# A quarter of the folded W_down summed elementwise ahead of its multiply, and first inputs loaded by halves on two queues, in a gated block with a decay scan and a gated MLP

## What is computed

```python
x = x + tanh(g_xattn[0]) * wkv(w, u, _layernorm(x), ctx)     # x, ctx: (8, 128, 256)
# wkv, for each batch and channel, over the 128 steps, in effect:
#   y_t = (sum_(s<t) e^((t-1-s) w + k_s) v_s + e^(u + k_t) v_t) / (the same without v)
x = x + tanh(g_ffn[0]) * ffn(_layernorm(x))
# ffn: a = fwht(n * SU_ug) / 64                                # 256 channels
#      h = silu(a @ W_gate.T * s_gate * 64) * (a @ W_up.T * s_up * 64)   # 1024 channels
#      out = fwht(h * SU_dp) / 64 @ W_down.T * (Wscale_dp * 64)
```

## Time and profile before

| | us |
|---|---|
| median of 3 runs | 106.79 |
| lowest, highest | 106.39, 107.57 |
| the profiled execution | 106.32 |
| its span | 104.4 |

### The profile page before, as it was taken

One profiled execution on the slowest core, in us unless ns is written; L12 is line 12 of the kernel. 1 busy time (PEld: TensorE's weight loads), 2 busy tenths in 40 slices (PEclk: granted clock), 3 DMA queues, 4 the chain that ended last, 5 costly groups with the idle time before them and its releaser, 6 DMA issues.

```text
span 104.4 us, 2022 instructions
## 1 busy us (share of the span) xinstructions
PE 95.8 (92%) x714; PEld 89.4 (86%) x714; DVE 70.2 (67%) x155; ACT 63.7 (61%) x140; POOL 52.3 (50%) x75
## 2 busy tenths in 40 slices
PE   0189999999999999999999999999999999999990
PEld 0148788759688999999999999999999999999980
DVE  0389989979999987999995689795325331412341
ACT  4497837978968744999477168937546432234310
POOL 5068697331999079530724927076493234322310
PEclk9999999999999999999999999999999999999999
DMA  1998999910000000000002000000200000020002
GB/s 58 293 272 257 397 393 401 365 71 6 0 0 0 0 6 0 0 0 0 0 0 105 5 0 0 0 9 0 100 0 0 0 6 0 0 100 0 0 0 100
DMA packets 3585, 7.69 MB, mean 74 GB/s; under 512 B 340, under 2 KB 760, under 8 KB 3576
## 3 DMA queue, kind: packets, MB, share of 16 engines
q1 hardware_dynamic: 3576, 7.57, 20.6%
HBM read 6.52 MB, written 1.05 MB: 73 GB/s over the span
## 4 chain that ended last, share of the span: by engine, by line
PE 86%; DMA 7%; SPq 3%; DVE 1%; issue 1%; DVEq 0%
PE UG L1046 45%; PE OD L1097 14%; PE KZ L1097 8%; DMA XT<-in_xt 7%; PE UG L961 3%; PE FX L1016 3%; PE FX L989 2%; PE UG L955 2%; PE FX L1001 2%; PE UG L975 1%; PE KZ L925 1%; PE UG L940 1%; PE VB L1026 1%; PE VB L1031 1%; PE VB L1038 1%
## 5 line engine op out<-in xcount | busy, mean ns | idle before, releaser
L437 POOL TENSOR_TENSOR HL<-H,HH 128x256 fp32r<-128x256 f32 x31 | 24.8, 807 | 27.6 <-ACT HH L703 27.6
L892 DVE SCALAR_TENSOR_TENSOR H<-S,ALPHA,UG 128x256 f32<-128x256 f32 x32 | 15.3, 478 | 19.0 <-ACT S L712 18.9
L712 ACT ACTIVATE S<-UG,CV 128x256 f32<-128x256 f32 x32 | 15.1, 472 | 13.5 <-PE UG L1046 13.5
L1046 PE MATMUL UG<-FH,WTH 128*128 128x256 f32 x128 | 21.8, 292 | 0.2 <-DVE FH L856 0.2
L1046 PE MATMUL UG<-FL,WTH 128*128 128x256 f32 x128 | 21.0, 286 | 0.0
L1046 PE MATMUL UG<-FH,WTL 128*128 128x256 f32 x128 | 20.5, 283 | 0.0
L1046 PEld LDWEIGHTS UG<-FH,WTH 128*128 128x128 f32 x128 | 17.7, 191 | 1.6 <-issue 0.8
L1046 PEld LDWEIGHTS UG<-FL,WTH 128*128 128x128 f32 x128 | 17.7, 191 | 0.5 <-issue 0.5
L1046 PEld LDWEIGHTS UG<-FH,WTL 128*128 128x128 f32 x128 | 17.6, 191 | 0.0
L703 ACT ACTIVATE HH<-H 128x256 fp32r<-128x256 f32 x32 | 13.2, 413 | 2.8 <-DVE H L892 2.6
L1097 PE MATMUL OD<-HH,MH 128*128 128x256 f32 x40 | 11.3, 283 | 0.0
(11 more groups left out here) (145 smaller groups left out, 191.1 us busy)
## 6 DMA issues: line engine op xcount, KB each, us to landing
WN<-in_weights SPq DMA_DIRECT2D x4, 512.0 KB, 9.4
DN<-in_w_down SPq DMA_DIRECT2D x2, 512.0 KB, 8.5
out<-XT SPq DMA_DIRECT2D x3, 256.0 KB, 2.4
X<-in_x SPq DMA_DIRECT2D x2, 256.0 KB, 3.4
V<-in_ct SPq DMA_DIRECT2D x2, 256.0 KB, 6.8
XT<-in_xt SPq DMA_DIRECT2D x2, 256.0 KB, 8.8
V<-in_ct SPq DMA_DIRECT2D x1, 512.0 KB, 9.2
X<-in_x SPq DMA_DIRECT2D x1, 512.0 KB, 10.4
```

Of the source, the lines that this page charges most:

```text
L437: eng.tensor_tensor(HL[:, q % JT, 0:n], ring(H, q), HH[:, q % JT, 0:n].bitcast(F32), ALU.subtract).then_inc(done, 1)
L712: act.activation(ring(S, q), gate_part(q), ACT.Silu, scale=VT[:, V_SGATE + j:V_SGATE + j + 1]).then_inc(silu_ready, 1)
L892: dve.scalar_tensor_tensor(out=ring(H, q), in0=ring(S, q), scalar=ALPHA[:, j:j + 1], in1=up_part(q), op0=ALU.mult, op1=ALU.mult).then_inc( ...
L1046: return pe.matmul(dst, w[:, m, j, t, :], f[:, g, t, :], start=start, stop=stop, skip_group_check=True)
```

## The change

SUMMED gets the second quarter: fly(9) is made, and its two matmuls become one. The lists of all four engines are reordered, before block 0 and up to block 22. x of group 0 and the constants are loaded in two halves by partitions, one from SP and one from ScalarE, and SP's later loads change their order. All waits on const_in and on x_in of group 0 ask for both halves; only two of them are shown.

```diff
@@ -42,15 +42,15 @@
 
 TURNED = (0, 1,)
 
-SUMMED = (2, 3)
+SUMMED = (1, 2, 3)
 
 LATE = (SLOTS - 1,)
 
 
 PE_STAGES = {
-    -1: [("busy", 0), ("center", 0), ("keys", 0), ("busy", 1), ("busy", 2), ("w", 0), ("fwht_x", 0), ("busy", 3), ("busy", 4),
-        ("keys", 1), ("w", 1), ("w_rest", 0), ("busy", 5), ("w", 2), ("fwht", 0), ("w", 3), ("w_rest", 1), ("ones", 0), ("m", 0),
-        ("spread", 0), ("w_rest", 2), ("w_rest", 3)],
+    -1: [("busy", 0), ("busy", 1), ("center", 0), ("keys", 0), ("w", 0), ("fwht_x", 0), ("busy", 2), ("busy", 3), ("w", 1), ("w", 2),
+        ("keys", 1), ("w_rest", 0), ("busy", 4), ("w_rest", 1), ("busy", 5), ("fwht", 0), ("w", 3), ("ones", 0), ("w_rest", 2), ("m", 0),
+        ("spread", 0), ("w_rest", 3)],
     0: [("keys", 2), ("m", 1)],
     2: [("m", 2)],
     3: [("m", 3)],
@@ -61,61 +61,61 @@
     12: [("fwht", 2)],
     13: [("ones", 2)],
     14: [("spread", 2)],
-    20: [("fwht", 3)],
-    21: [("ones", 3)],
-    22: [("spread", 3)],
+    18: [("fwht", 3)],
+    19: [("ones", 3)],
+    20: [("spread", 3)],
 }
 ACT_STAGES = {
-    -1: [("setup", 0), ("rows", 0), ("signs", 0), ("steps", 0), ("tanh", 0), ("decay", 0), ("keys", 0), ("gated", 0), ("ratio", 0),
-        ("recip", 0), ("w_hi", 0), ("w_lo", 0), ("keys", 1), ("w_hi", 1), ("w_hi", 2), ("square", 0), ("w_hi", 3), ("w_hi", 4),
-        ("f_copy", 0), ("w_hi", 5), ("w_lo", 1), ("w_lo", 2), ("w_lo", 3), ("m_hi", 0), ("norm1", 2), ("recip", 1), ("keys", 2)],
+    -1: [("setup", 0), ("rows", 0), ("tanh", 0), ("signs", 0), ("steps", 0), ("decay", 0), ("keys", 0), ("ratio", 0), ("recip", 0),
+        ("w_hi", 0), ("w_hi", 1), ("w_hi", 2), ("gated", 0), ("keys", 1), ("square", 0), ("w_lo", 0), ("w_hi", 3), ("w_hi", 4),
+        ("f_copy", 0), ("w_lo", 1), ("w_lo", 2), ("w_lo", 3), ("norm1", 2), ("recip", 1), ("m_hi", 0), ("keys", 2)],
     0: [("m_hi", 1)],
-    3: [("m_hi", 2), ("m_hi", 3), ("x_hi", 1), ("w_hi", 6), ("w_hi", 7), ("square", 1)],
-    5: [("f_copy", 1), ("f_hi", 1)],
-    7: [("norm1", 3), ("exp_block", (("keys", 3), ("recip", 2)))],
+    1: [("w_hi", 5)],
+    2: [("m_hi", 2), ("m_hi", 3)],
+    3: [("x_hi", 1), ("w_hi", 6), ("w_hi", 7), ("square", 1), ("f_copy", 1)],
+    4: [("norm1", 3)],
+    5: [("f_hi", 1)],
+    7: [("exp_block", (("keys", 3), ("recip", 2)))],
     9: [("x_hi", 2)],
     11: [("square", 2)],
     12: [("f_copy", 2)],
-    13: [("f_hi", 2)],
-    15: [("exp_block", (("recip", 3),))],
-    17: [("x_hi", 3)],
-    19: [("square", 3)],
-    20: [("f_copy", 3)],
+    13: [("exp_block", (("recip", 3),)), ("f_hi", 2)],
+    16: [("x_hi", 3), ("square", 3)],
+    19: [("f_copy", 3)],
     22: [("f_hi", 3)],
 }
 DVE_STAGES = {
-    -1: [("stats1", 0), ("alpha", 0), ("setup_rows", 0), ("norm1", 0), ("stats1", 1), ("center", 0), ("scan_a", 0), ("av", 0),
-        ("mix_den", 0), ("scan_av", 0), ("mix_num", 0), ("estimate", 0), ("newton", 0), ("fly", 1), ("fly", 3), ("scan_a", 1),
-        ("fly", 6), ("fly", 5), ("var", 0), ("stats1", 2), ("f_scaled", 0), ("outs", 0), ("f_lo", 0), ("mix_den", 1), ("fly", 7),
-        ("x1", 0), ("av", 1), ("m_lo", 0), ("scan_av", 1)],
-    0: [("m_lo", 1), ("mix_num", 1)],
+    -1: [("stats1", 0), ("setup_rows", 0), ("outs", 0), ("alpha", 0), ("norm1", 0), ("stats1", 1), ("center", 0), ("scan_a", 0),
+        ("av", 0), ("mix_den", 0), ("scan_av", 0), ("mix_num", 0), ("estimate", 0), ("newton", 0), ("fly", 1), ("fly", 3), ("scan_a", 1),
+        ("fly", 6), ("var", 0), ("stats1", 2), ("mix_den", 1), ("f_scaled", 0), ("f_lo", 0), ("fly", 7), ("av", 1), ("m_lo", 0),
+        ("x1", 0), ("scan_av", 1)],
+    0: [("m_lo", 1), ("fly", 11), ("mix_num", 1)],
     1: [("estimate", 1)],
-    2: [("newton", 1), ("x1", 1), ("m_lo", 2), ("x_lo", 1), ("w_lo", 6), ("w_lo", 7)],
-    3: [("stats1", 3), ("var", 1)],
-    4: [("av", 2), ("m_lo", 3), ("f_scaled", 1)],
-    5: [("f_lo", 1)],
-    6: [("scan_a", 2), ("mix_den", 2), ("scan_av", 2)],
-    7: [("mix_num", 2), ("error", 2), ("estimate", 2)],
-    8: [("newton", 2)],
-    9: [("x1", 2), ("av", 3), ("x_lo", 2)],
-    13: [("var", 2), ("scan_a", 3), ("f_scaled", 2), ("mix_den", 3), ("f_lo", 2)],
-    14: [("scan_av", 3), ("mix_num", 3), ("estimate", 3)],
-    15: [("error", 3)],
-    16: [("newton", 3)],
-    17: [("x1", 3)],
-    20: [("var", 3)],
-    22: [("f_scaled", 3), ("f_lo", 3)],
+    2: [("newton", 1), ("x1", 1), ("m_lo", 2), ("x_lo", 1), ("stats1", 3)],
+    3: [("m_lo", 3), ("w_lo", 7), ("var", 1)],
+    4: [("scan_a", 2)],
+    5: [("f_scaled", 1), ("av", 2), ("f_lo", 1)],
+    7: [("scan_av", 2), ("mix_den", 2), ("mix_num", 2), ("av", 3), ("error", 2), ("estimate", 2), ("newton", 2)],
+    8: [("x1", 2)],
+    10: [("scan_a", 3)],
+    12: [("mix_den", 3), ("var", 2), ("scan_av", 3), ("f_scaled", 2)],
+    13: [("mix_num", 3), ("f_lo", 2), ("error", 3)],
+    14: [("estimate", 3), ("newton", 3)],
+    15: [("x1", 3), ("x_lo", 3)],
+    18: [("var", 3)],
+    21: [("f_scaled", 3)],
+    22: [("f_lo", 3)],
 }
 POOL_STAGES = {
     -1: [("rstd1", 0), ("setup_shift", 0), ("rstd1", 1), ("norm1", 1), ("fly", 0), ("error", 0), ("fly", 2), ("fly", 4), ("rstd2", 0),
-        ("rstd1", 2), ("fly", 10), ("error", 1), ("fly", 11), ("w_lo", 5), ("w_lo", 4)],
-    1: [("sum", 1)],
-    2: [("rstd2", 1), ("rstd1", 3)],
+        ("rstd1", 2), ("fly", 5), ("fly", 9), ("fly", 10), ("error", 1), ("w_lo", 5), ("w_lo", 4)],
+    1: [("w_lo", 6), ("sum", 1), ("rstd1", 3)],
+    2: [("rstd2", 1)],
+    8: [("x_lo", 2)],
     9: [("sum", 2)],
-    11: [("rstd2", 2)],
-    16: [("x_lo", 3)],
-    17: [("sum", 3)],
-    19: [("rstd2", 3)],
+    10: [("rstd2", 2)],
+    15: [("sum", 3)],
+    17: [("rstd2", 3)],
 }
@@ -449,7 +449,9 @@
             def load_x(i):
                 b = slice(GB * i, GB * (i + 1) if i < 2 else NB)
-                sp.dma_start(X[:, b, :], x[:, b, :]).then_inc(x_in[i], 16)
+
+                p = slice(0, P if i else P // 2)
+                sp.dma_start(X[p, b, :], x[p, b, :]).then_inc(x_in[i], 16)
...
             def load_consts():
-                sp.dma_start(CV[:, :], consts).then_inc(const_in, 16)
+                sp.dma_start(CV[0:P // 2, :], consts[0:P // 2, :]).then_inc(const_in, 16)
...
             load_x(0)
+            load_consts()
             load_rows()
-            load_consts()
             load_steps()
             load_x(1)
             load_ctx(0)
             load_w(0)
             load_xt(0)
             load_down(0)
+            load_w(1)
             load_down(1)
+            load_x(2)
+            load_w(2)
             load_ctx(1)
-            load_w(1)
+            load_w(3)
             load_ctx(2)
-            load_w(2)
-            load_x(2)
             load_xt(1)
-            load_w(3)
             load_xt(2)
...
                 if name == "setup":
+                    act.dma_start(X[P // 2:, 0:GB, :], x[P // 2:, 0:GB, :]).then_inc(x_in[0], 16)
+                    act.dma_start(CV[P // 2:, :], consts[P // 2:, :]).then_inc(const_in, 16)
                     act.preload_act_table_set("exp_and_others")
...
-                    dve.wait_ge(x_in[arrival(g)], 16)
+                    dve.wait_ge(x_in[arrival(g)], 16 if g else 32)
...
-                    pe.wait_ge(const_in, 16)
+                    pe.wait_ge(const_in, 32)
```

More of the change, by code:

```diff
@@ L603, in stage @@
                 elif name == "signs":
-                    act.wait_ge(const_in, 16)
+                    act.wait_ge(const_in, 32)
                     for o in range(CT):
@@ L752, in stage @@
                 elif name == "outs":
-                    dve.wait_ge(const_in, 16)
+                    dve.wait_ge(const_in, 32)
                     dve.wait_ge(tanh_gate, 2)
```

12 lines of the change are left out of this document (6 added, 6 removed).

## The result

The changed kernel is slower: 110.41 us (median of 4 runs, 109.09 to 111.65) against 106.75 us (4 runs, 106.39 to 107.57) for the kernel before on the same chip. The ratio is 1.028, 95% interval 1.0223 to 1.0336. The profiled execution took 109.09 us with a span of 107.3 us; before it was 106.32 and 104.4 us. I had forecast 106.7 us and no change.

A forecast was written before the change was run, and what follows sets the result against it. TensorE, 92% busy, was taken to bound the kernel once XT arrives. 106.32 + 0.38 - 0.25 + 0, plus 0.1 for small stalls, gave 106.55 us; between that and 0.47 more, the median was placed at 106.7, range 105.5 to 108.0.

The forecast's parts named there:

- part 3: Loads of x of group 0 and constants by halves on two queues: XT 0.25 us earlier.
- the clock that I left as it was in the sum: TensorE's clock before block 0: risen by about 8.2 us, L989 fast, no term; a late rise would cost +1.0 to +2.0.
- Bounds: at least, nothing: Limits on the gain from halved loads: at most 0.5 us earlier for all queued behind, at least nothing.
- Rival C: TensorE before block 0: clock rises late for want of work between 8.2 and 11 us; 107.55 to 108.55 us, chance 0.22.
- the gap of 0.18 us: TensorE's one idle gap from 8.60 us on in the kernel before; its clock was said to rise after it.
- One sign that I named: Sign of a late clock: L989 and busy matmuls behind it at twice their time, block 0 starting at 23.5 us or later.
- Part 2: TensorE's new order before block 0: XT's arrival to end of L1001 goes from 7.08 to 7.46 us, +0.38.
- Behind L1001 nothing gets longer: Between L1001 and t0, the start of block 0, the reordered work adds no time.
- Part 1: Second quarter by sum: m(1) 0.89 us shorter, all turned into TensorE waits before group 1's fwht; net 0 after block 0's start.
- Rival B: The gain of the shorter m(1) is kept: 105.75 us, or 105.5 with all of the loads' gain; chance 0.22.
- the 69.5 us from the fwht of group 1 to the end: Time from group 1's fwht to the end of the span, claimed to stay as in the kernel before.
- The wait of 0.3 us that I feared in stage 13: Possible wait in groups 1 to 3; f_lo 2, behind two table loads, was tightest, with some 0.3 us or more found.

The follow-up runs named there:

- b_fillers_early: Kernel before with two busy matmuls moved from between keys 0 and w 0, one ahead of center, one behind L989; 108.65 us.
- a_whole: Changed kernel with x of group 0 and the constants loaded whole by SP, in the order x, rows, constants; 107.48 us, ratio 1.005.
- a_whole_two: Changed kernel with whole loads from SP, without fly 9, the second quarter by two matmuls as before; 108.17 us.

## Why the prediction was wrong

Three steps failed: the -0.25 us of part 3, the clock that I left as it was in the sum, and the nothing that I put for the time behind the fwht of group 1.

**Part 3, two queues: the step that failed first.** I took half of the 0.54 us unused by the DMA engines as a gain, -0.25 us, with nothing as the worst case. Measured alone on before it is +0.8 us in the medians (in the profile L989 starts at 12.06 us for 11.17), and taking it out of the changed kernel gives 2.9 us back. I priced a half's issue with the row of a whole, about 0.36 us, and read the unused DMA time as room. It did not fill: the halves made SP's issues later, and between 2 and 4 us the engines were less busy than before. In the changed kernel's profile what came late by that was the first pair of weights (0.6 us), and XT by only 0.1. "Bounds: at least, nothing" had no row behind it; the only issue rows were of whole transfers.

**The clock: right mechanism, wrong weight.** Rival C had the place, the cause and the size: L989 at +1.03 us, the low end of my 1.0 to 2.0. I gave it 0.22. With the loads of before eight of eleven executions of b_fillers_early lie in the upper group, so 0.22 was too low even without the halves; in a_whole it is two of ten, and what sets the share stays open. I also had the rise behind the gap of 0.18 us, where it was ahead of it, within w 0. One sign that I named was not met: the busy matmuls behind L993 were fast already, since the clock rose within it. t0 at 23.5 us or later was met, at 24.52.

**Part 2: right.** From the start of L989 to the end of L1001 I had 7.08 and 7.46 us. In a_whole, where the clock is no matter, the chain has 10.43 to 17.94, 7.51 us; in the changed kernel 8.47, of which 1.03 is the clock. "Behind L1001 nothing gets longer" missed 0.23 us: the ones matmuls stand closer behind their input, wait 0.13 us and take 1.04 instead of the 0.92 us of the chain before.

**Part 1: right, with two small misses.** The whole 0.89 us of m(1) is eaten before the fwht of group 1: t0 + 12.29, for 12.24 before. It is eaten on the path that I named. In the changed kernel's timeline of VectorE and TensorE, m(2), block 4 and the second half of the fwht each start 0.05 to 0.07 us behind the end of the first hidden product, the third, and x_lo 1:

```profile
30.55 0.48 DVE L896 SCALAR_TENSOR_TENSOR H<-S,ALPHA,UG 128x256 f32<-128x256 f32 x1 [0.55 <-ACT S L716]
31.10 1.11 PE L959 MATMUL UG<-DB,CV 128*128 128x512 f32 x2
...
34.02 0.47 DVE L896 SCALAR_TENSOR_TENSOR H<-S,ALPHA,UG 128x256 f32<-128x256 f32 x1
34.54 0.74 PE L1050 MATMUL UG<-FH,WTH 128*128 128x256 f32 x4
...
36.58 0.69 DVE L413 TENSOR_TENSOR XL<-XT,XH 128x512 fp32r<-128x512 f32 x1
37.33 0.74 PE L1020 MATMUL FX<-XL,AT 128*128 128x256 f32 x4
```

I had that second half at t0 + 12.87; it starts at t0 + 12.81. The waits behind m(1) are some 0.4 us together and not 0.6 to 0.9, since the wait for fly 9 took the rest. Fly 9 took 1.29 us for my 1.3. TensorE's wait for it was 0.42 us and not 0.1, since fly 7 ended at t0 + 2.24 (I had 2.05) and 0.14 us passed from the end of fly 9 to m(1); as the whole gain was to go anyway, this changed nothing. Rival B is out: 0.06 us in a_whole_two.

**After group 1: the step that I left out.** I took the 69.5 us from the fwht of group 1 to the end as fixed. It is 70.5 now (82.78 less 12.29; 81.85 less 12.24, or 69.6, before). I looked at the moved operations by their distance to their own readers, w_lo 5 to 7 and f_lo 2, and did not follow rstd2 1, which was not moved but got an operation put ahead of it. The wait of 0.3 us that I feared in stage 13 did not form in the profile; the wait that did stands on GpSimd, the engine that the page shows half idle. It accounts for 0.60 of the 0.93 us; what holds the rest, and holds it when this wait is undone, stays open.

With the five measured pieces the sum is 106.32 + 0.34 + 1.03 + 0.37 + 0.23 + 0.93 = 109.22 us; the profiled run took 109.09 us, as its ends around the span are 0.1 us shorter. The median of 110.41 us lies 1.3 us above that run, and this part no profile explains.
